# Two attention layers on one core: the value products of two score blocks in one bank, the output projections one a step, and the transposes of one residual block a step sooner

## The chip, the cores and the metric
One core of a Trainium2 chip runs the whole kernel. The metric is the device time in microseconds (us), from one launch; lower is better.

## The reference
The input x is 128 sequences of 128 tokens and 256 features, float32, with one 128x128 integer adjacency matrix for each sequence. Two layers follow each other:

```python
# layer 0: pre-norm transformer block, 8 heads of 32
nx = ln(x) * g1 + b1
scores = q @ k.T / sqrt(32) + where(adj > 0, 0.1 * adj * adj, -inf)
x1 = x + softmax(scores) @ v @ wo + bo
x2 = x1 + gelu(ln(x1) @ w1 + b1) @ w2 + b2          # 256 -> 1024 -> 256
# layer 1: graph attention, post-norm
scores = q @ k.T / sqrt(32), -inf where adj == 0
out = ln(x2 + softmax(scores) @ v @ Wo + bo) * gamma + beta
```

## The kernel before, in words
The 128 sequences go in 32 groups of 4 (GB). A software pipeline of 34 turns works on three groups at a time: stage A (attention of layer 0) on group i, stage M (the MLP of layer 0) on group i-1, stage C (layer 1) on group i-2. Turns 2 to 30 are one hardware loop of 29 turns; turns 0, 1, 31, 32 and 33 are written out, with some stages missing. `make_shapes` (L160) builds the turns and `Shape` (L73) the order of the work within one.

A turn has eight steps. Each step takes one score block (one sequence): steps 0 to 3 those of stage C (C0 to C3), steps 4 to 7 those of stage A (A0 to A3). What belongs to a score block is spread over several steps, on five engines:

- Scores: TensorE multiplies queries by keys in 32-row tiles (`make_scores` L1200, products at L1217). VectorE adds the mask and takes the negative maximum (L864), ScalarE exponentiates (L651), VectorE inverts the sums (`invert` L869) and GpSimd multiplies by them (`make_probs` L580, products at L585), in two halves of four heads, called g0 and g1.
- T, one step later: TensorE transposes the probabilities (`turn` L1221), half g0 before and half g1 after the output projection; ScalarE copies g0 out (L683), VectorE g1 (L923). A transpose waits for the GpSimd product of its half.
- V, two steps later: the products with the values in 32-column tiles (L1249), 16 records a block. ScalarE makes the rounded part (`heads_high` L685) and VectorE the remainder (`heads_low` L925), each 256 columns wide.
- W, also two steps later: the output projection in three passes (L1258), then residual and layer norm statistics on VectorE (`add_residual`, `measure`) and the reciprocal root on GpSimd (`rstd_of` L552).
- One step after W of a block of C: normalise on VectorE (`apply_norm` L949), gamma and beta on GpSimd (`finish` L566, L572 and L574), then SP stores the block (`store` L471).

Each engine has its own instruction queue and runs it in the order written in `body`; semaphores join them. TensorE's order in a step is: scores, V, the ops of `early` and `mid`, T g0, W, T g1, the ops of `ahead` (transposes of a residual block, XT), the ops of `fill`. Those tables (L105 to L111) hold the large products: K and Q of A and V of A in steps 0 to 2, up projection and first half of the down projection in step 3, second half in step 4, K, Q and V of C in steps 5 to 7. XT N, the transposes of the next group's normalised input, stand in step 7.

GpSimd's order in a step is at L579 to L625. At step 0 it first waits until all blocks of C of the turn before are stored, adds the bias of C to half a group (L593), then makes the g1 product of step 7's block, then the second half of the bias, then the g0 product of step 0's block:

```python
if k == 0 and s.c:
    wait(pool, stored, t.group_c * GB * 16)
    ...add_bias("C", drained[bank], number, 0, 1)
if k in s.open:
    make_probs(k - 1, 1)
...
for r in s.late.get(k, []):
    finish(t, r)
...
if k == 7 and s.a:
    add_bias("A", res_a_loaded, (t.group_a + 1) * 16, 1, 1)
rstd_of(t, s.lag.get(k, []))
```

Results of TensorE go through four PSUM banks in turn (`Turn.bank`), whose numbering follows TensorE's order.

Of the kernel before, what the change touches and what calls it, by code (L numbers as in the profile page):

```python
# [54 lines left out]
LOW_STEPS = {0: {5: [3], 6: [4], 7: [5]}, 1: {4: [6], 5: [7]}}  # L55
# [4 lines left out]
def lags(steps, pending, drain):  # L60

    by_step = {}
    for r, k in enumerate(steps):
        by_step[k] = ([("V", r - 2), ("W", r - 2)] if r >= 2 or pending else []) + (
            [("T", r - 1)] if r >= 1 or pending else [])
    last = len(steps) - 1
    tail = [("V", last - 1), ("T", last), ("W", last - 1), ("V", last), ("W", last)] if drain else []
    return by_step, tail  # L70


class Shape:  # L73
# [3 lines left out]
    def __init__(self, it, stages, following, before, drain):  # L77
# [13 lines left out]
        self.late, waiting = {}, [-3] if pending else []  # L91
        for k in self.steps:
# [6 lines left out]
                     if ((k - 1 in self.units and k - 1 != self.behind) if k != self.steps[0] else pending)]  # L99
# [9 lines left out]
        fill = {0: [("K", "A", 1)], 1: [("Q", "A", 1)], 2: [("V", "A", 1)],  # L109
# [3 lines left out]
        self.early = {k: [early[k]] for k in present if k in early}  # L113
        self.mid = {k: mid[k] for k in present if k in mid}
        self.fill = {k: fill[k] for k in present if k in fill}
        if before is None:

            self.early.update({5: [("XT", "N")], 6: [("K", "N", 1)], 7: [("Q", "N", 1)]})
            self.fill[1].append(("BIAS", 1))
            self.fill.update({5: [("K", "N", 0)], 6: [("Q", "N", 0)]})  # L120
            self.fill[7] = [("BIAS", 7)]
            self.tail = self.tail[:1] + [("BIAS", 2)] + self.tail[1:-1] + [
                ("V", "N", 0), self.tail[-1], ("V", "N", 1), ("BIAS", 3)]
# [14 lines left out]
        assert not self.looped or len(self.use) % BANKS == 0  # L138

# [30 lines left out]
class Turn:  # L170
# [28 lines left out]
    def normed_room(self, what):  # L199

        return (self.it + (what in "MN")) % 2
# [22 lines left out]
def build(nc, T, out):  # L224
    ctx = ExitStack()
    with ctx:
# [26 lines left out]
        probs_t = sb("probs_t", [P, H, P])  # L253
        heads_t = sb("heads_t", [P, 2, KC, P], F32R)
        piece_rooms = [sb(f"piece_room{i}", [P, 2, TOK]) for i in range(4)]
        scaled_rooms = [sb(f"scaled_room{i}", [P, 2, TOK]) for i in range(2)]
# [75 lines left out]
        scaled = [as_piece(scaled_rooms[n % 2][:, :, :]) for n in range(8)]  # L332
# [80 lines left out]
        def turned_rows(g):  # L413

            return probs_t[:, HC * g:HC * (g + 1)].rearrange("p (a h) n -> p a (h n)", a=2)
# [5 lines left out]
        def made(t, kind, what, i):  # L421
# [4 lines left out]
            return t.bank((kind, what, i), earlier=(what == "C"))  # L426
# [11 lines left out]
        def _(sp):  # L438
# [36 lines left out]
            def body(t):  # L475
# [26 lines left out]
                if s.c:  # L502
                    store(t, 0)
                    store(t, 1)
# [3 lines left out]
                if s.c:  # L508
                    store(t, 2)
# [11 lines left out]
        def _(pool):  # L521
# [11 lines left out]
            def scale_later(n):  # L533

                pool.wait_ge(piece_loaded[n], 16 * len(pieces[n][0]))
                if n in scaled_later:
                    pool.wait_ge(piece_done, EARLY_PIECES)
                    scale_part(nc.gpsimd, n).then_inc(later_scaled, 1)
# [37 lines left out]
            def body(t):  # L576
                s = t.s
                setup_over(pool, t)
                for k in range(STEPS):  # L579
# [16 lines left out]
                    for n in steps_of(LOW_STEPS, t).get(k, []):  # L596
# [18 lines left out]
                    rstd_of(t, s.lag.get(k, []))  # L615
                    if k == 3 and s.following and s.before is not None:
# [13 lines left out]
        def _(act):  # L630
# [49 lines left out]
            def turned(t, r):  # L680
                u, _, _ = t.unit(r)
                act.wait_ge(probs_turned, u * KC + 1)
                nc.scalar.activation(turned_rows(0), turned_columns(0), ACT.Copy).then_inc(turned_out0, 1)  # L683

            def heads_high(t, r):  # L685
                bank, number = t.bank(("O", r))
                act.wait_ge(filled[bank], number)
                nc.scalar.activation(heads_t[:, HI].rearrange("p c n -> p (c n)"), p_bank[bank][:, 0:KC * P],  # L688
                                     ACT.Copy).then_inc(high_made, 1)

            def body(t):
                s = t.s
                setup_over(act, t)
                for k in range(STEPS):
# [15 lines left out]
                    for _, r in only("T", lag):  # L710
                        turned(t, r)
                    if k in s.units and k != s.behind and not long:
                        exps(t, k, 1)
                    for op in s.ahead.get(k, []):
# [599 lines left out]
```

## Time and profile before

| what | value |
|---|---|
| time, median of 3 runs | 2192.55 us (2192.16 to 2194.01) |
| the profiled execution's own time | 2193.79 us |
| its span, first to last instruction | 2191.2 us |
| mean granted TensorE clock | 0.991 of full speed |
| TensorE busy | 2148.5 us, 98% |
| VectorE / ScalarE / GpSimd busy | 82% / 77% / 53% |
| one turn of the loop, from scores to scores | 66.12 us (1012.84 to 1078.96) |

The page gives busy time by engine and the costliest groups of instructions. Times in a timeline count from the span's start. In it a row is a run of equal instructions: start, time from the first start to the last end, engine, line, what is written and read, how many, and in brackets the idle time before it. TensorE's matmuls overlap, so the distance from one row's start to the next row's start is what a block of them costs, not its own duration.

### The profile page before, as it was taken

How to read it: one execution, taken by the hardware profiler on the slowest of the kernel's cores; microseconds unless marked ns; L12 is line 12 of the kernel's file. 1: busy time of each engine (PE TensorE's matmuls, PEld its weight loads, DVE VectorE, ACT ScalarE, POOL GpSimd, SP SyncE). 2: the span in 40 equal slices, each digit the busy share in tenths (PEclk: the TensorE clock that was granted, in tenths of full speed). 3: DMA queues.
4: the chain of work that ended last, by engine and by line, in shares of the span. 5: the costliest groups of instructions: out<-in, count | busy, mean ns of one | idle time of the engine just before them, and what ended most of it. 6: DMA issues, size and time to landing. Idle time of an engine off the chain costs nothing.

```text
span 2191.2 us, 58906 instructions
## 1 busy us (share of the span) xinstructions
PE 2148.5 (98%) x20300; PEld 1858.1 (85%) x20300; DVE 1798.5 (82%) x8414; ACT 1682.8 (77%) x5646; POOL 1153.9 (53%) x1266
## 2 busy tenths in 40 slices
PE   8899999999999999999999999999999999999986
PEld 6788888888888888888888888888888888888875
DVE  6588888888888888888888888888888888888774
ACT  5578777778877778877787877787877787877773
POOL 4345655455555455555455555455554456554454
PEclk9899999999999999999999999999999999999998
DMA  4010111001110101111101110101110101110000
GB/s 128 25 34 30 40 33 36 27 28 38 38 35 30 33 26 39 33 40 31 30 28 40 33 40 26 34 28 40 33 40 25 35 28 40 33 40 23 26 16 18
DMA packets 94308, 75.74 MB, mean 35 GB/s; under 512 B 8128, under 2 KB 93760, under 8 KB 94016
## 3 DMA queue, kind: packets, MB, share of 16 engines
q1 hardware_dynamic: 94016, 71.99, 10.9%
q8 instruction: 166, 2.72, 0.5%
q14 instruction: 126, 1.03, 0.2%
HBM read 55.20 MB, written 16.78 MB: 33 GB/s over the span
## 4 chain that ended last, share of the span: by engine, by line
PE 95%; issue 2%; DVE 1%; ACT 1%; POOL 0%; DMA 0%; SPq 0%; POOLq 0%; DVEq 0%
PE p_bank L1133 66%; PE p_heads L1230 10%; PE p_heads L1217 8%; PE p_bank L1249 7%; PE p_bank L1152 4%; ACT scores L651 1%; DVE normed L886 0%; DVE probs_t L923 0%; PE p_bank L1062 0%; DMA scores<-in_L_gnn_wk 0%; PE p_bank L1088 0%; POOL res_a L563 0%; SPq L442 0%; ACT normed L662 0%; ACT heads_t L688 0%
## 5 line engine op out<-in xcount | busy, mean ns | idle before, releaser
L651 ACT ACTIVATE scores<-scores,negmax 128x128 f32<-128x128 f32 x2048 | 793.7, 392 | 18.3 <-DVE negmax L864 18.0
L585 POOL TENSOR_TENSOR scores<-scores,inverse 128x512 f32<-128x512 f32 x512 | 541.2, 1062 | 329.9 <-DVE inverse L875 329.9
L651 ACT ACTIVATION_READ_ACCUMULATOR scores<-scores,negmax 128x1 f32 x2048 | 391.9, 191 | 0.0
L1133 PEld LDWEIGHTS p_bank<-w_down,hidden 128*128 128x128 f32 x3072 | 374.8, 190 | 8.6 <-issue 5.9
L1133 PE MATMUL p_bank<-w_down,hidden 128*128 128x256 f32 x3072 | 381.9, 284 | 0.0
L1133 PE MATMUL p_bank<-normed,w_up 128*128 128x512 f32 x1536 | 369.9, 397 | 2.2 <-DVE normed L886 2.2
L1133 PEld LDWEIGHTS p_bank<-normed,w_up 128*128 128x128 f32 x1536 | 284.9, 189 | 67.5 <-issue 8.6
L1230 PE MATMUL p_heads<-ident,scores 128*128 128x128 f32 x2048 | 312.7, 276 | 6.9 <-DVE negmax L864 3.5
L864 DVE CUSTOM_DVE_ANT_0 scores<-p_heads,adj_a 128x128 f32<-128x128 f32 x1024 | 235.2, 286 | 45.2 <-issue 45.2
L674 ACT ACTIVATE p_bank<-p_bank,ready_cols 128x512 f32<-128x512 f32 x256 | 169.5, 662 | 132.2 <-PE p_bank L1133 126.5
L1230 PEld LDWEIGHTS p_heads<-ident,scores 128*128 128x128 f32 x2048 | 241.5, 141 | 32.9 <-DVE negmax L864 10.5
L864 DVE CUSTOM_DVE_ANT_0 scores<-p_heads,adj_c 128x128 f32<-128x128 f32 x1024 | 233.2, 286 | 36.1 <-issue 36.1
L1133 PE MATMUL p_bank<-w_o,heads_t 128*128 128x256 f32 x1536 | 246.5, 296 | 1.9 <-DVE heads_t L929 1.9
L910 DVE TENSOR_TENSOR hidden<-p_bank,hidden 128x512 fp32r<-128x512 f32 x256 | 177.1, 692 | 63.0 <-ACT hidden L678 57.1
L688 ACT ACTIVATE heads_t<-p_bank 128x256 fp32r<-128x256 f32 x256 | 98.3, 384 | 166.7 <-PE p_bank L1249 166.7
L683 ACT ACTIVATE probs_t<-p_heads 128x512 f32<-128x512 f32 x256 | 149.9, 585 | 89.3 <-PE p_heads L1230 89.3
L530 POOL TENSOR_TENSOR rstd_A<-spread_A,half 128x4 f32<-128x4 f32 x32 | 32.5, 1017 | 352.2 <-DVE spread_A L765 352.2
L1133 PE MATMUL p_bank<-normed,w_k 128*128 128x512 f32 x768 | 211.4, 412 | 5.1 <-DVE normed L886 3.9
L1133 PE MATMUL p_bank<-normed,w_q 128*128 128x512 f32 x768 | 210.5, 410 | 0.0
L1133 PE MATMUL p_bank<-w_v,normed 128*128 128x256 f32 x1536 | 209.8, 287 | 0.0
L1133 PEld LDWEIGHTS p_bank<-w_o,heads_t 128*128 128x128 f32 x1536 | 199.7, 191 | 3.0 <-DVE heads_t L929 2.8
L1133 PEld LDWEIGHTS p_bank<-w_v,normed 128*128 128x128 f32 x1536 | 186.7, 189 | 12.6 <-issue 12.5
(117 smaller groups left out, 3698.1 us busy)
## 6 DMA issues: line engine op xcount, KB each, us to landing
res_a<-in_x SPq DMA_DIRECT2D x32, 512.0 KB, 3.8
out<-res_c SPq DMA_DIRECT2D x128, 128.0 KB, 1.7
x_in<-in_x SPq DMA_DIRECT2D x31, 512.0 KB, 3.8
adj_a<-in_adj SPq DMA_DIRECT2D x32, 256.0 KB, 2.9
adj_c<-in_adj SPq DMA_DIRECT2D x32, 256.0 KB, 2.8
piece_room<-in_L_gnn_w SPq DMA_DIRECT2D x2, 512.0 KB, 7.5
x_two<-in_x SPq DMA_DIRECT2D x1, 512.0 KB, 5.4
res_c<-in_L_gnn_w SPq DMA_DIRECT2D x1, 512.0 KB, 6.3
```

The lines of the kernel that those rows point to most:

```text
L585: nc.gpsimd.tensor_tensor(rows_g, rows_g, inverse[:, step % 2, heads].unsqueeze(2).broadcast_to([P, HC, P]), ALU.mult).then_inc(probs_made, 1)
L651: last = nc.scalar.activation(scores[:, k % 2, h], scores[:, k % 2, h], ACT.Exp, scale=-1.0, bias=negmax[:, k % 2, h:h + 1], accum_out=tot ...
L674: nc.scalar.activation(src[:, :], src[:, :], ACT.Gelu, bias=ready_cols[:, 8 + j:9 + j]).then_inc(gelu_made, 1)
L683: nc.scalar.activation(turned_rows(0), turned_columns(0), ACT.Copy).then_inc(turned_out0, 1)
L688: nc.scalar.activation(heads_t[:, HI].rearrange("p c n -> p (c n)"), p_bank[bank][:, 0:KC * P], ACT.Copy).then_inc(high_made, 1)
L864: nc.vector.tensor_tensor_reduce(out=scores[:, k % 2, slot], in0=score_columns(c, j), in1=adj[stage][:, b, :], scale=1.0, scalar=LARGEST, ...
L910: nc.vector.tensor_tensor(hidden[:, j, LO, :], src[:, :], hidden[:, j, HI, :].bitcast(F32), ALU.subtract).then_inc(drained[bank], 1)
L1133: last = nc.tensor.matmul(dst, stationary(i), moving(j), start=(n == 0), stop=(n == total_n - 1))
L1152: last = nc.tensor.transpose(dst[:, b * P:(b + 1) * P], src[:, b, c * P:(c + 1) * P], ident[:, :])
L1217: last = nc.tensor.matmul(score_columns(c, j), queries[room(t, stage)][rows_j, c, tokens], keys[room(t, stage)][rows_j, c, tokens], start= ...
L1230: last = nc.tensor.transpose(turned_columns(g)[:, n // 2, (n % 2) * P:(n % 2 + 1) * P], scores[:, par, HC * g + n, :], ident[:, :])
L1249: last = nc.tensor.matmul(dst[HD * j:HD * (j + 1), c * P:(c + 1) * P], values[room(t, stage)][:, b, h * HD:(h + 1) * HD], probs_t[:, slot_ ...
```

## The change
The value products of two blocks are made one after the other in the steps 1, 3, 5 and 7 into one bank, 512 columns wide, and rounded and subtracted at that width; `probs_t` and `heads_t` become double. W is done for the blocks of `W` in the table:

| step | before: V, W | after: V | after: W |
|---|---|---|---|
| 0 | A2 | none | A1 |
| 1 | A3 | A2, A3 | A2, A3 |
| 2 | C0 | none | none |
| 3 | C1 | C0, C1 | C0 |
| 4 | C2 | none | C1 |
| 5 | C3 | C2, C3 | C2 |
| 6 | A0 | none | C3 |
| 7 | A1 | A0, A1 | A0 |

(The A blocks of steps 0 and 1 are those of the turn before.) `finish` and the norm of a block of C move with its W: C3's from step 6 to step 7. XT N moves from step 7 to step 6, both halves of V of A stand in `early` of step 2, ScalarE evacuates XT before the second half of its exponentials, and SP stores block 1 behind the load of `res_a`. At the ends: V of C for the last group moves from turn 32 into the first step of turn 33; in turn 0 V of A moves behind the first scores; in turn 1 GpSimd scales and splits the last two weight pieces in steps 2 and 3 instead of 4 and 5; the drained tails are reordered. GpSimd's order in a loop turn is otherwise the same.

```diff
+    by_step = {k: [] for k in steps}
     for r, k in enumerate(steps):
-        by_step[k] = ([("V", r - 2), ("W", r - 2)] if r >= 2 or pending else []) + (
-            [("T", r - 1)] if r >= 1 or pending else [])
+        by_step[k] += [("T", r - 1)] if r >= 1 or pending else []
+        by_step[k] += [("W", -3)] if r == 0 and pending else []
+        if r % 2 and (r >= 3 or pending):
+            by_step[k] += [("V", (r - 3, r - 2)), ("W", r - 3)]
+            if r == 1:
+                by_step[k] += [("W", r - 2)]
+            elif r < len(steps) - 1:
+                by_step[steps[r + 1]] += [("W", r - 2)]
-    tail = [("V", last - 1), ("T", last), ("W", last - 1), ("V", last), ("W", last)] if drain else []
+    tail = [("W", last - 2), ("V", (last - 1,)), ("T", last), ("W", last - 1), ("V", (last,)), ("W", last)] if drain else []
...
-                      7: [("XT", "N")] * (a and following and before is not None)}
-        early = {1: ("Q", "A", 0), 2: ("V", "A", 0), 4: ("DOWN", 1), 6: ("Q", "C", 0), 7: ("V", "C", 0)}
+                      6: [("XT", "N")] * (a and following and before is not None)}
+        early = {1: [("Q", "A", 0)], 2: [("V", "A", 0), ("V", "A", 1)], 4: [("DOWN", 1)], 6: [("Q", "C", 0)],
+                 7: [("V", "C", 0)]}
...
+        if it == NG:
+            del self.early[7], self.fill[7]
+        if it == NG + 1:
+            self.early[0], self.fill[0] = [("V", "C", 0)], [("V", "C", 1)]
         if before is None:
+            del self.early[2]
+            self.fill[4] = [("V", "A", 0), ("V", "A", 1)]
...
-            def heads_high(t, r):
-                bank, number = t.bank(("O", r))
+            def heads_high(t, units):
+                bank, number = t.bank(("O", units))
                 act.wait_ge(filled[bank], number)
-                nc.scalar.activation(heads_t[:, HI].rearrange("p c n -> p (c n)"), p_bank[bank][:, 0:KC * P],
+                nc.scalar.activation(heads_part(HI, units), p_bank[bank][:, 0:len(units) * KC * P],
                                      ACT.Copy).then_inc(high_made, 1)
...
+                    if k == 2 and second_turn(t):
+                        scale_later(6)
...
+                    if k == 3 and second_turn(t):
+                        low_later(6)
+                        scale_later(7)
+                        low_later(7)
```

## Rows read from the trace of the kernel before
**Rows 1.** Windows: one turn; busy us of each engine, granted clock, DMA share, GB/s.
```profile
1012.84:1078.96 66.12, 66.08 (x633) 57.38 (x633) 55.91 (x263) 52.25 (x178) 35.50 (x39) 1.00 0.11 33
```
**Rows 2.** Timeline, TensorE: from step 6 to step 0 of the next turn.
```profile
1032.37 0.60 PE L1230 MATMUL p_heads<-ident,scores 128*128 128x128 f32 x4
...
1034.29 0.73 PE L1217 MATMUL p_heads<-keys_a,queries_a 32*128 32x128 f32 x16
...
1038.59 1.04 PE L1152 MATMUL p_bank<-ident,x_in 128*128 128x128 f32 x8
1039.38 1.62 PE L1133 MATMUL p_bank<-w_v,normed 128*128 128x256 f32 x12
1040.94 0.73 PE L1217 MATMUL p_heads<-keys_c,queries_c 32*128 32x128 f32 x16
1041.60 0.64 PE L1249 MATMUL p_bank<-probs_t,values_a 128*32 128x128 f32 x16
1042.17 1.65 PE L1133 MATMUL p_bank<-normed,w_k 128*128 128x512 f32 x6
...
1044.81 0.60 PE L1230 MATMUL p_heads<-ident,scores 128*128 128x128 f32 x4
```
**Rows 3.** Timeline, TensorE, turn 1: step 4, and a wait after it.
```profile
83.53 0.73 PE L1217 MATMUL p_heads<-keys_a,queries_a 32*128 32x128 f32 x16
84.19 6.02 PE L1133 MATMUL p_bank<-w_down,hidden 128*128 128x256 f32 x48
...
94.16 0.66 PE L1152 MATMUL p_bank<-ident,x_two 128*128 128x128 f32 x4 [3.52 <-DVE x_two L917]
```
**Rows 4.** Timeline, ScalarE: step 7 of the same turn.
```profile
1035.66 0.38 ACT L688 ACTIVATE heads_t<-p_bank 128x256 fp32r<-128x256 f32 x1 [0.57 <-PE p_bank L1249]
...
1037.96 0.58 ACT L683 ACTIVATE probs_t<-p_heads 128x512 f32<-128x512 f32 x1
```
**Rows 5.** The page, part 5: VectorE subtractions, 512 and 256 wide; busy us, mean ns.
```profile
L910 DVE TENSOR_TENSOR hidden<-p_bank,hidden 128x512 fp32r<-128x512 f32 x256 | 177.1, 692 | 63.0 <-ACT hidden L678 57.1
...
L929 DVE TENSOR_TENSOR heads_t<-p_bank,heads_t 128x256 fp32r<-128x256 f32 x256 | 107.2, 419 | 24.3 <-ACT heads_t L688 24.2
```
**Rows 6.** Timeline, GpSimd: steps 5 to 0 of the same turns.
```profile
1026.75 1.12 POOL L585 TENSOR_TENSOR scores<-scores,inverse 128x512 f32<-128x512 f32 x1 [0.34 <-DVE inverse L875]
1027.83 0.73 POOL L572 TENSOR_TENSOR res_c<-res_c,gamma 128x256 f32<-128x256 f32 x1
...
1029.32 1.28 POOL L563 TENSOR_TENSOR res_a<-res_a,row_bias 128x512 f32<-128x512 f32 x1
...
1031.08 2.10 POOL L585 TENSOR_TENSOR scores<-scores,inverse 128x512 f32<-128x512 f32 x2
...
1037.87 1.04 POOL L585 TENSOR_TENSOR scores<-scores,inverse 128x512 f32<-128x512 f32 x1 [0.64 <-DVE inverse L875]
1038.87 1.29 POOL L563 TENSOR_TENSOR res_a<-res_a,row_bias 128x512 f32<-128x512 f32 x1
1040.31 0.55 POOL L530 TENSOR_TENSOR rstd_M<-spread_M,half 128x1 f32<-128x1 f32 x1
1040.82 1.27 POOL L563 TENSOR_TENSOR res_c<-x_two,row_bias 128x512 f32<-128x512 f32 x1
...
1042.91 1.04 POOL L585 TENSOR_TENSOR scores<-scores,inverse 128x512 f32<-128x512 f32 x1 [0.81 <-DVE inverse L875]
```
**Rows 7.** Timeline, GpSimd: beta of a block, then a bias that waits for its store.
```profile
2145.26 0.72 POOL L574 TENSOR_TENSOR res_c<-res_c,beta 128x256 f32<-128x256 f32 x1
2147.77 2.54 POOL L563 TENSOR_TENSOR res_c<-x_two,row_bias 128x512 f32<-128x512 f32 x2 [1.78 <-DMA out<-res_c]
```
**Rows 8.** Timeline, TensorE: rows after waits, in turns 0, 32 and 33.
```profile
52.21 1.08 PE L1230 MATMUL p_heads<-ident,scores 128*128 128x128 f32 x4 [1.40 <-issue]
...
2103.40 0.73 PE L1217 MATMUL p_heads<-keys_c,queries_c 32*128 32x128 f32 x16 [1.72 <-DVE probs_t L923]
...
2158.73 0.73 PE L1217 MATMUL p_heads<-keys_c,queries_c 32*128 32x128 f32 x16 [1.91 <-DVE negmax L864]
```

More of the change, by code:

```diff
@@ L88, in __init__ @@
         self.lag, self.tail = lags(self.steps, pending, drain)
-        self.late, waiting = {}, [-3] if pending else []
+        self.pending = pending
+        self.late, waiting = {}, []
         for k in self.steps:
@@ L138, in __init__, with use_units @@
         assert not self.looped or len(self.use) % BANKS == 0
+    def use_units(self, r):
+        return [use[1] for use in self.use if use[0] == "O" and use[1][0] == r]
     def number(self, ops):
@@ L199, in normed_room @@
     def normed_room(self, what):
-        return (self.it + (what in "MN")) % 2
+        return (self.it + (what in "MN" or not self.s.m and self.s.c)) % 2
     def high(self, key):
@@ L331, in build @@
                                         piece_rooms[3][:, :, :])]
-        scaled = [as_piece(scaled_rooms[n % 2][:, :, :]) for n in range(8)]
+        scaled = [as_piece(scaled_room[:, :, :]) for n in range(8)]
         w1, w2 = w_view(L0 + "w1"), w_view(L0 + "w2")
@@ L425, in made, with second_turn @@
                 return t.bank((kind, "N", i), earlier=True)
-            return t.bank((kind, what, i), earlier=(what == "C"))
+            return t.bank((kind, what, i), earlier=(what == "C" and not (kind == "V" and t.it == NG + 1)))
+        def second_turn(t):
+            return t.s.before is not None and t.s.before.before is None
         def steps_of(table, t):
@@ L508, in body @@
                 if s.c:
+                    store(t, 1)
                     store(t, 2)
@@ L595, in body @@
                         make_probs(k - 1, 1)
-                    for n in steps_of(LOW_STEPS, t).get(k, []):
+                    for n in LOW_STEPS.get(k, []) if s.before is None else []:
                         if n > 3:
@@ L711, in body @@
                         turned(t, r)
+                    for op in s.ahead.get(k, []) if not long else []:
+                        evacuate(t, op)
                     if k in s.units and k != s.behind and not long:
                         exps(t, k, 1)
-                    for op in s.ahead.get(k, []):
+                    for op in s.ahead.get(k, []) if long else []:
                         evacuate(t, op)
@@ new lines, in project @@
+            def project(t, r):
+                for units in t.s.use_units(r):
+                    bank, number = t.bank(("O", units))
+                    pe.wait_ge(drained[bank], number)
+                bank, dst = take(t, ("W", r))
+                w = weight[weights_of[t.unit(r)[1]][3]]
+                three_passes(dst[:, 0:D], [(lambda i, c=c: heads_t[:, i, parity(r), c, :], lambda j, c=c: w[:, j, c, :])
+                                           for c in range(KC)]).then_inc(filled[bank], 1)
@@ L1236, in lagging @@
+            def lagging(t, op, which):
                 if op == "T":
                     for g in range(2):
-                        turn(t, r, g)
+                        turn(t, which, g)
                 if op == "V":
-                    bank, dst = take(t, ("O", r))
-                    pe.wait_ge(turned_out0, u + 1)
-                    pe.wait_ge(turned_out1, u + 1)
-                    if b == 0:
-                        for i in range(2):
-                            pe.wait_ge(*drained_bank(*made(t, "V", stage, i)))
@@ L1246, in lagging @@
[L1246 to L1260 removed]
+                    value_products(t, which)
```

93 lines of the change are left out of this document (48 added, 45 removed).

## The prediction
> **What bounds the kernel now.** I read the windows first, one turn of the loop: TensorE is busy 66.08 of 66.12 us, at granted clock 1.00, which is the upper of its two levels, 2.4 GHz; VectorE, ScalarE and GpSimd are busy 55.91, 52.25 and 35.50 us [rows 1]. So in the 29 loop turns nothing but TensorE's own queue sets the time, and every microsecond that this queue waits is paid in full. Then I read TensorE's timeline row by row for what a block of each kind costs (start to next start), and at last the timelines of GpSimd and ScalarE for how long before its use each result is ready. The reader should look in the last for slack: a product of the probabilities that ends shortly before the transpose that needs it.
>
> **What TensorE saves.** A block of value products costs 0.57 us (1041.60 to 1042.17) [rows 2]. Eight 128-column transposes take 1.04 us in their row and four take 0.60, so one more costs 0.11; a block is four rounds of four tiles side by side, 0.44 us if they ran at that pitch. The missing 0.13 is the change of tile shape and is paid once a block. A pair then costs 0.57 + 0.44 = 1.01 us and not 1.14. Where V goes from a step altogether, the scores are followed by the next full-size product after 0.66 us (83.53 to 84.19) [rows 3], the same 0.66 as from scores to V (1040.94 to 1041.60) [rows 2], so V is taken out whole. Four pairs a turn: 4 x 0.13 = 0.54 us with the unrounded starts. Bounds: nothing, if each block keeps its own 0.13; 4 x 0.2 = 0.8, if the pair also hides some of what surrounds it. I take 0.54, since the rows give it directly. W, T and XT keep their number and widths; joining or parting them shifts less than 0.1 us a turn either way, which I set to nothing. Over 31 turns that have pairs: -17 us.
>
> **What the other engines save.** ScalarE and VectorE do four wide roundings for eight narrow ones. On ScalarE a 256-wide copy takes 0.38 and a 512-wide one 0.58 [rows 4]; on VectorE 0.42 and 0.69 [rows 5]. All of it lies beside TensorE, so it buys nothing; but each wide one is longer, and what is queued behind it comes later.
>
> **What becomes late: T g1 in step 0.** Let zero be the start of the scores of step 7 (1034.29). Before, T g1 of step 0 starts at 10.52 (1044.81) [rows 2]. The product of GpSimd that it needs (g1 of step 7's block) starts at 8.62 (1042.91) and ends at 9.66 [rows 6]: slack 0.86. After the change TensorE comes sooner: XT N has left step 7 (-0.79, 1038.59 to 1039.38 [rows 2]), the pair is +0.44, V has left step 0 (-0.57): it wants T g1 at 10.52 - 0.92 = 9.60.
> GpSimd comes later, step by step [rows 6, 4]:
> the g0 product of step 7 starts at 3.58 (1037.87); it waits for the inverse of sums whose exponentials stand behind `heads_high` on ScalarE. The pair ends 0.44 later and its copy is 0.20 longer (0.58 for 0.38): 4.22.
> It occupies 1.00 (1037.87 to 1038.87): 5.22.
> `finish` of C3 is new here, since C3's W moved from step 5 to step 6: gamma and beta occupy 1.49 (1027.83 to 1029.32): 6.71.
> The bias of A, 1.29: 8.00. The reciprocal root, 0.51 (1040.31 to 1040.82): 8.51. Before there was 0.15 of idle time ahead of it, now none.
> In step 0 GpSimd waits until C3 is stored. From the end of beta (2145.98) to the bias that its store releases (2147.77) it is 1.79 us [rows 7]: 6.71 + 1.79 = 8.50, by chance the same moment.
> The bias of C, 1.27, stands ahead of the product: 9.78. The product, 1.04: 10.82, plus some 0.03 for the semaphore.
> T g1 waits 10.85 - 9.60 = 1.25 us. The 0.82 us that GpSimd had waited for the inverse before its product [rows 6] are used up in this count. Behind T g1 on TensorE stand K of A, the scores of step 1 and everything else, with no other work to fill the gap. Bounds: 0.6 if GpSimd's small instructions and the store are quicker than in these rows; 2.0 if ScalarE, which now evacuates XT N before the second half of its exponentials, gets late too. The store's size is the least certain term.
> The Trainium skill, "DMA: Bandwidth & Descriptors", in "Anatomy of one DMA — SWDGE (gpsimd) path", gives a fixed cost of about 2.0 us a DMA, most of it the wait for the write to be confirmed; the trace has 1.79 us with beta's hand-over in it [rows 7], for a DMA issued by SP. With 2.0 the wait would be an estimated 1.5 us and the sum 6 us more; the measured one is used.
>
> **What becomes late: T g1 in step 6.** GpSimd's queue from the g0 product of step 5 (1026.75) to the g1 product at 1031.08 has no gap: product, `finish`, bias of A, root, product. That first product waits for an inverse behind the masks and `heads_low`, now 0.69 - 0.42 = 0.27 longer [rows 5], so the g1 product ends at 1032.12 + 0.27 = 1032.39. T g1 stood at 1032.37 [rows 2], with 0.25 of slack, and moves by +0.44 - 0.57 to 1032.24. That is 0.15 of wait, and up to 0.4 where K of C in step 5 no longer waits for its transposes. I take 0.3. Both waits come in 30 turns: the first at the starts of turns 3 to 32, the second in turns 2 to 31. Together 30 x 1.55 = +46 us.
>
> **The edits of W, XT M and V of A** are covered: W of a pair's first block stands 1.9 us behind the pair (a K, Q or V product and T g0), against 1.3 us for the two wide roundings; XT M reaches the up projection behind scores and a pair, 1.7 us, for the roundings of two banks.
>
> **The ends.** In turn 1 TensorE waits 3.52 us for the down projection's sum [rows 3], because ScalarE's exponentials stand behind weight pieces that GpSimd scales in step 4; scaled two steps sooner they don't: -3.5, and an estimated -1.5 for the products behind it, which after such gaps at the ends can run at the lower clock (T in 1.08 for 0.60 at 52.21 [rows 8]). V of C placed behind the first scores of turn 33 covers the 1.91 us wait [rows 8]: -1.9; V of A likewise in turn 0, where I take a little less: -1.5. The drained tail now has W of one more block, so after the last root GpSimd finishes four blocks and not three: +1.5 (1.49 as above). Sum -7, between -14 and +2.
>
> **Sum.** Against the profiled execution's own time, 2193.8 (its span is 2191.2): 2193.8 - 17 + 46 - 7 = 2216. The median of the runs shown is 1.2 us lower, so 2215 us.
>
> **Rivals.**
> A, faster: GpSimd is ready in time. The time is 2192.6 - 17 - 7 = 2168 us. For it: GpSimd is idle for 30 of 66 us of a turn [rows 1]. Against: that idle time lies in steps 3 and 4; between step 7's g0 product and step 0's g1 product it has 0.97 us of it (0.15 and 0.82), while 1.49 of `finish` and 0.64 of delay are added. It decides if that product ends 9.6 us after the scores of step 7.
> B, in between: the two waits add up to 0.4 to 1.0 us a turn; the change breaks even at 24 / 30 = 0.8. 2180 to 2199, middle 2190.
> C, much slower: the new gap lowers TensorE's clock in each turn. After 1.40 us of waiting four transposes took 1.08 us in place of 0.60 (52.21) [rows 8]: if some 2.5 us a turn are lost so, 2215 + 75 = 2290. Against: after waits of 1.72 and 1.91 us the scores ran in 0.73 us, as at full clock (2103.40, 2158.73) [rows 8], and here 9 us of dense products stand ahead of the gap.
> [...]
> D, the pair doesn't save: each block keeps its 0.13. Then 2215 + 17 = 2232.
>
> **Chances.** Forecast 0.66, A 0.15, B 0.10, C 0.05, D 0.04. The measurement tells no change from a change within 0.2%, 4.4 us: 2188 to 2197. Faster: A and a third of B, 0.18. Same: half of B, 0.05. Slower: the rest, 0.77. The forecast's own range is 2199 to 2234. To leave out no more than A and C the range starts in B, at 2180, and ends at 2236, with D in it.
>
> **What would show it.** In TensorE's timeline: rows of 32 value products costing 1.01 us, and steps 0, 2, 4 and 6 without any (D: 1.14). Rows of transposes in step 0 with about 1.25 us of idle time, in step 6 with 0.3; in the waits, GpSimd's probabilities as a releaser that isn't there now. A turn of 67.1 us, not 66.12 (A: 65.6). On GpSimd gamma and beta between step 7's product and the bias of A, and the bias of C of step 0 at 8.5 us after the scores of step 7. Granted clock 1.00 over a turn; below 0.97 would be C. The first 100 us some 6 us shorter. I would be wrong if GpSimd's bias of C started before 7.2 us, or if another engine waited instead.

## The result, and the profile after

| | before | after |
|---|---|---|
| time, median | 2193.39 us (2192.16 to 2194.01) | 2254.04 us, 5 runs (2248.59 to 2258.19) |
| ratio, 95% interval | | 1.0268 (1.0252 to 1.0284) |
| span of the profiled execution | 2191.2 us | 2255.7 us (its own time 2258.2) |
| mean granted TensorE clock | 0.991 | 0.985 |
| a turn | 66.11 to 66.16 us, the last of them 65.24 | 67.57 us in 19 of 30, 66.30 in one, 68.3 to 70.4 in ten |

The change makes the kernel 61 us slower. The forecast said slower by 22, and its range (2180 to 2236) doesn't hold the result. The profiled execution of the kernel after was the slowest of its five, so the spans differ by 64.5 us and the medians by 60.7.

One thing has to be put right first. The text ahead of the prediction says that turns 2 to 30 are one hardware loop. They are not: `make_shapes` (L160) writes all 34 turns out one after the other. That matters below: the profile shows 165 fetches of instructions, 16 KB each, spread over the whole span (queue q8).

The windows of the kernel after, in the columns of [rows 1]: a common turn, a long one, and eight microseconds of the long one.

```profile
998.24:1065.81 67.57, 66.03 (x633) 57.64 (x633) 55.78 (x258) 51.74 (x173) 35.42 (x40) 1.00 0.11 33
314.07:383.93 69.86, 67.55 (x634) 58.67 (x633) 55.78 (x258) 51.74 (x173) 35.44 (x40) 0.98 0.10 32
318.00:326.00 8.00, 6.29 (x63) 4.78 (x64) 4.19 (x18) 3.35 (x14) 5.35 (x6) 0.79 0.16 55
```

TensorE was busy all of the turn before (66.08 of 66.12); now 1.54 us of the common turn are idle. Its timeline, from step 6 to step 0 of the next turn, answers to [rows 2]:

```profile
1056.78 0.63 PE L1267 MATMUL p_heads<-ident,scores 128*128 128x128 f32 x4
...
1059.60 0.73 PE L1255 MATMUL p_heads<-keys_a,queries_a 32*128 32x128 f32 x16
1060.26 1.08 PE L1285 MATMUL p_bank<-probs_t,values_a 128*32 128x128 f32 x32
1061.27 1.65 PE L1171 MATMUL p_bank<-w_v,normed 128*128 128x256 f32 x12
...
1063.11 0.96 PE L1171 MATMUL p_bank<-w_o,heads_t 128*128 128x256 f32 x6
1063.90 0.60 PE L1267 MATMUL p_heads<-ident,scores 128*128 128x128 f32 x4
...
1065.81 0.73 PE L1255 MATMUL p_heads<-keys_c,queries_c 32*128 32x128 f32 x16
...
1068.32 0.95 PE L1171 MATMUL p_bank<-w_o,heads_t 128*128 128x256 f32 x6
1070.68 0.63 PE L1267 MATMUL p_heads<-ident,scores 128*128 128x128 f32 x4 [1.41 <-issue]
1071.07 1.64 PE L1171 MATMUL p_bank<-normed,w_k 128*128 128x512 f32 x6
```

The pair costs 1.01 us (1060.26 to 1061.27). W costs 0.79 (1063.11 to 1063.90), so TensorE wanted T g1 of step 0 at 1069.11, 9.51 after step 7's scores; it starts at 11.08, 1.57 late. GpSimd's timeline of the same stretch answers to [rows 6]:

```profile
1063.83 1.12 POOL L617 TENSOR_TENSOR scores<-scores,inverse 128x512 f32<-128x512 f32 x1 [1.29 <-DVE inverse L916]
1064.92 0.74 POOL L604 TENSOR_TENSOR res_c<-res_c,gamma 128x256 f32<-128x256 f32 x1
1065.73 0.73 POOL L606 TENSOR_TENSOR res_c<-res_c,beta 128x256 f32<-128x256 f32 x1
1066.42 1.29 POOL L595 TENSOR_TENSOR res_a<-res_a,row_bias 128x512 f32<-128x512 f32 x1
1067.67 0.55 POOL L561 TENSOR_TENSOR rstd_M<-spread_M,half 128x1 f32<-128x1 f32 x1
1068.31 1.28 POOL L595 TENSOR_TENSOR res_c<-x_two,row_bias 128x512 f32<-128x512 f32 x1
1069.55 1.04 POOL L617 TENSOR_TENSOR scores<-scores,inverse 128x512 f32<-128x512 f32 x1
```

Seven operations in a row with no gap over 0.1 us, and T g1 waits for the last. In a long turn the same two places (GpSimd, then TensorE) read:

```profile
317.35 1.26 POOL L595 TENSOR_TENSOR res_c<-x_two,row_bias 128x512 f32<-128x512 f32 x1 [0.87 <-DMA out<-res_c]
```
```profile
319.71 0.66 PE L1267 MATMUL p_heads<-ident,scores 128*128 128x128 f32 x4 [2.18 <-issue]
320.10 2.83 PE L1171 MATMUL p_bank<-normed,w_k 128*128 128x512 f32 x6
```

Here GpSimd waits 0.87 us for the store of the fourth block of C, TensorE waits 2.18, and then the six products of K take 2.83 us in place of 1.64 and the scores of step 1 behind them 1.05 in place of 0.73: the granted clock over 318 to 326 us is 0.79, so part of that stretch ran at the lower level of 1.2 GHz.

**Where the 64.5 us of span went**, from the starts of the scores: before turn 2, -2.6 (115.27 to 112.66); turns 2 to 31, +58.7, which is +42.3 for turns longer by 1.45 and +16.4 more in ten of them; turn 32 between its scores 0 and 3, +8.2 (15.03 to 23.23); the rest +0.2.

The ten long turns are just those whose store lands late. The fourth block's store is issued 0.68 us after the scores of step 0 every time. In turns 3 to 31 it lands 1.75 us later in 19 and takes 2.47 to 3.22 in ten; in turn 32 it is late too (2.85). In six of the ten the turn is longer by exactly what the store is late, within 0.02 (landed 3.22, so 1.47 late: turn 69.04, 1.47 longer). In the other four it is 1.5 longer still (landed 2.54, 0.79 late: turn 69.85, 2.28 longer), which is K and the products behind it at the lower clock.

### The profile page after: what moved, and what is told of

Its sections match the earlier page's. It is cut to its first block, busy times and chain, and to the rows that moved or that the text cites. A ratio compares the mean times of both kernels' runs of the same rounds, so it can differ in the third digit from the quotient of the medians.

```text
span 2255.7 us, 58407 instructions
## 1 busy us (share of the span) xinstructions
PE 2157.7 (96%) x20300; PEld 1873.5 (83%) x20300; DVE 1798.8 (80%) x8289; ACT 1666.3 (74%) x5521; POOL 1153.1 (51%) x1266
## 3 DMA queue, kind: packets, MB, share of 16 engines
q14 instruction: 124, 1.02, 0.2%
## 4 chain that ended last, share of the span: by engine, by line
PE 92%; issue 4%; DVE 1%; ACT 1%; POOL 0%; POOLq 0%; DVEq 0%; ACTq 0%
PE p_bank L1171 64%; PE p_heads L1267 10%; PE p_heads L1255 7%; PE p_bank L1285 6%; PE p_bank L1190 4%; ACT scores L689 0%; DVE probs_t L964 0%; DVE scores L905 0%; POOL res_c L604 0%; DVE normed L927 0%; DVE heads_t L969 0%; POOL res_c L606 0%; ACT normed L700 0%; DVE res_c L979 0%; DVE stats_C L797 0%
## 5 line engine op out<-in xcount | busy, mean ns | idle before, releaser
L1171 PE MATMUL p_bank<-w_o,heads_t 128*128 128x256 f32 x1536 | 239.0, 295 | 3.5 <-DVE heads_t L969 3.5
L964 DVE COPY probs_t<-p_heads 128x512 f32<-128x512 f32 x256 | 176.7, 690 | 60.3 <-PE p_heads L1267 58.7
L1171 PE MATMUL p_bank<-normed,w_k 128*128 128x512 f32 x768 | 217.0, 420 | 3.4 <-DVE normed L927 3.4
L1171 PE MATMUL p_bank<-w_v,normed 128*128 128x256 f32 x1536 | 203.5, 285 | 0.0
```

The lines of the kernel that those rows point to most:

```text
L964: nc.vector.tensor_copy(turned_rows(r, 1), turned_columns(1)).then_inc(turned_out1, 1)
L1171: last = nc.tensor.matmul(dst, stationary(i), moving(j), start=(n == 0), stop=(n == total_n - 1))
```

## The experiments

"The turn" is the common turn in the middle of the kernel. All runs are compared with the kernel before on their own chip.

**e1: the product ahead of the bias.** GpSimd makes the g1 product of step 7's block before it waits for the store.

```diff
+                    if k in s.open:
+                        make_probs(k - 1, 1)
                     if k == 0 and s.c:

                         wait(pool, stored, t.group_c * GB * 16)
                         bank, number = t.bank(("DOWN", 1), earlier=True)
                         add_bias("C", drained[bank], number, 0, 1)
-                    if k in s.open:
-                        make_probs(k - 1, 1)
```

> The changed kernel, with one edit: in step 0 GpSimd makes the g1 product of step 7's block before it waits for the stores and adds the bias of C. Theory Q (GpSimd's queue): the product starts when the root ends, 8.6 us after the scores of step 7, and T g1 waits 0.2 in place of 1.56 us; but the bias of C now ends 1.0 us later, VectorE's normalisation of block A0 waits for it with the copy of T g1 behind it, and the scores of step 1 wait for that copy: 0.8 to 1.2 us come back there. A turn of 67.1 to 67.4 us (67.57 now); the turns with a late store lose most of their excess, since the bias has 0.9 us to spare. Time 2230 to 2240 us. Rival (TensorE is held by the product alone): a turn of 66.2 us, time 2205 us.

Measured: 2252.07 us, ratio 1.0263 (1.0248 to 1.0278), turn 67.85. A miss: T g1 is only 0.2 late, but the scores of step 1 now wait 1.58, more than the 0.8 to 1.2 expected. From the waits of this run (who waited for whom; total us, times, longest):

```profile
PE p_heads L1255 <- DVE probs_t L964: 54.3, 34, 3.0
...
DVE x_two L811 <- POOL res_c L595: 46.9, 31, 2.0
```

VectorE's norm of a residual block overwrites `x_two`, which the bias of C must have read; behind the norm on VectorE stands the copy of T g1's bank, and the next scores need that bank. So two chains hang on the same late moment of GpSimd, 31 times each; mending one of them gives nothing that these runs can tell (2 us, with ranges that overlap).

**e2: no wait for the store.** The sum of C goes to a weight room that is free by then, so GpSimd no longer waits for the store, and VectorE's move of the first block of C, in a later step, waits for it instead.

```diff
-                x, src = (res_c, x_two) if stage == "C" else (res_a, res_a)
+                x, src = (sum_c, x_two) if stage == "C" else (res_a, res_a)
...
-                        wait(pool, stored, t.group_c * GB * 16)
...
+                if stage == "C" and b == 0:
+                    wait(dve, stored, t.group(r) * GB * 16)
```

> The changed kernel, with the sum of x2 and the bias of C written to a free weight room and not over the block being stored, so that GpSimd waits for no store in step 0 (VectorE waits for it in step 3, long after). Order of the queues as in the changed kernel. Theory Q: the common turn stays at 67.5 us, since the root ends only 0.1 us before the store lands; what goes is the excess of the turns with a late store (15.5 us in all in the profiled run) and about 2 us of the wait in turn 32: time 2233 to 2240 us. Rival S (the store is what TensorE waits for): the whole 1.56 us a turn goes, 66.0 us a turn, time 2190 us.

Measured: 2230.46 us, ratio 1.0165 (1.0150 to 1.0181). Turns 3 to 30 are all 67.42 or 67.43; no long one is left.

```profile
982.90:1050.33 67.43, 66.02 (x634) 57.65 (x634) 55.77 (x258) 51.70 (x173) 35.36 (x40) 1.00 0.11 33
```

23.6 us of the 61 hang on the store and only 0.14 us of each common turn: with a store of 1.75 GpSimd is released at about the moment at which it comes free anyway.

**e3: loads behind the store.** SP waits for the store before it issues the loads of `adj_a` and `x_in`, which otherwise follow it within 1.4 us.

```diff
                 if s.c:
                     store(t, 3)
+                    sp.wait_ge(stored, (t.group_c + 1) * GB * 16)
```

> The changed kernel, with one edit: SP waits until C3 is stored before it issues the loads of adj_a and x_in, which now are issued 0.4 and 0.9 us behind that store. Theory V (a store's landing time varies by itself: in the trace of the kernel before 30 of 128 stores took over 2.0 us from issue, most with no load behind them): nothing changes, about a third of the turns keep their excess, time 2248 to 2258 us. Rival L (the loads delay the store): no late store in step 7, no turn over 67.6 us but for turn 32, time 2236 to 2240 us.

Measured: 2254.01 us, ratio 1.0270 (1.0252 to 1.0287), the same long turns at the same places. The loads don't make the late stores. They cost every store a little: without them behind it the punctual one takes 1.69 us, not 1.75, and the common turn is 67.51.

**e4: the late finish in the kernel before.** Gamma and beta of the fourth block of C in step 7 instead of step 6, nothing else.

```diff
                     for r in s.late.get(k, []):
-                        finish(t, r)
+                        if not (k == 6 and s.a and s.c):
+                            finish(t, r)
+                    if k == 7 and s.a and s.c:
+                        finish(t, 3)
```

> The kernel before, with one edit: gamma and beta of C3 in step 7 and not in step 6 (what the change does to GpSimd, without what it does to TensorE, ScalarE and VectorE). Theory Q: the bias of C starts 7.9 us after the scores of step 7, the g1 product ends at 10.2, T g1 stands at 10.5: the common turn keeps its 66.1 us. Theory V adds: a store that lands over 0.3 us late is now paid for, 9 to 15 us in all, time 2201 to 2208 us. Rival (the work put into step 7 is paid by itself): 1.2 us a turn, 2230 us. Rival L: 2193 us, since here the x load comes 4 us after that store.

Measured: 2197.82 us, ratio 1.0024 (1.0014 to 1.0034). That is less than the 2201 to 2208 expected. The common turn stays 66.12; five turns are 0.2 to 0.8 longer, and turn 32 between its scores 0 and 3 takes 19.25 for 15.03. The later finish alone is nearly free, because in the kernel before TensorE wants T g1 0.92 us later.

**e5: e2, and the finish deferred.** GpSimd's gamma and beta of the fourth block go behind all its work of step 0 of the next turn.

```diff
                     for r in s.late.get(k, []):
-                        finish(t, r)
+                        if not (k == 7 and r == 3 and not s.drain):
+                            finish(t, r)
...
                     rstd_of(t, s.lag.get(k, []))
+                    if k == 0 and s.before is not None and s.before.c and not s.before.drain:
+                        finish(t, 3, t.group_c - 1)
```

> The changed kernel with GpSimd's bias of C in a room of its own (as in e2), and the finish of the fourth block of C (the product with g1 is unchanged; its scale, gamma, beta and the store behind them) taken out of step 7's list on GpSimd and put behind all that GpSimd does in step 0 of the next turn. What is computed is the same. Theory Q (the cost of the turn is TensorE's wait for T g1's source in step 0, and that is late only because GpSimd's gamma and beta of the fourth block stand ahead of it): with some 1.9 us of work taken from ahead of it the bias of C starts early enough, the wait of 1.3 to 1.5 in step 0 is gone, and the turn falls from 67.43 to 66.0 (the wait of 0.3 in step 6 stays); 2230.5 less 31 times 1.4 gives 2187 (2184 to 2191). Rival R (another wait stands right behind, as in e1: VectorE's norm or the copies of the probabilities): the turn stays above 67.0 and the time at 2215 or more. The difference of the two is what one projection a step with pairs of value products costs beyond GpSimd's order.

Measured: 2198.70 us, ratio 1.0018 (1.0007 to 1.0028), turn 66.38. T g1 of step 0 is on time, but only 1.05 of the 1.4 us came back: the scores of step 1 now wait 0.33 for VectorE's copy.

**e6: e5, and the bias of A a step later.**

```diff
-                    if k == 5 and s.a:
+                    if k == (5 if s.before is None else 6) and s.a:
                         add_bias("A", res_a_loaded, (t.group_a + 1) * 16, 0, 1)
```

> e5, and in the full turns the bias of A's first half is done by GpSimd in step 6 and not in step 5. The change brought a wait of 0.3 for T g1 in step 6 as well, which I put to GpSimd's queue of step 5. Theory Q: it goes, the turn falls from 66.0 to 65.7, below the 66.12 of the kernel before by what the pairs save (4 times 0.13), and the time to 2178 (2174 to 2182). Rival R: the bias of A is wanted by the norm in step 6 itself, a wait of the same length takes its place, and the time stays at e5's within 3 us.

Measured: 2187.58 us, ratio 0.9971 (0.9961 to 0.9981), turn 66.03. The edit gives 0.35 a turn, the wait of step 6, as expected; the level is 0.35 too high, as in e5.

**e7: e6, and the last turn reordered.** GpSimd's part of it; on VectorE the norms stand ahead of the moves of the third and the fourth block.

```diff
-                        rstd_of(t, s.tail)
-                        for r in s.last:
-                            finish(t, r)
+                            rstd_of(t, tail_w[:1])
+                            finish(t, s.last[0])
+                            finish(t, s.last[1])
+                            rstd_of(t, tail_w[1:2])
+                            finish(t, s.last[2])
+                            rstd_of(t, tail_w[2:])
+                            finish(t, s.last[3])
```

> e6, and in the last turn VectorE's norms and GpSimd's finishes of the four blocks are taken in the order in which their projections end, in place of all roots first and all finishes behind. Theory: at the end of the changed kernel four finishes stand in a row behind the last projection (from last W to end 11.2 us), of which two can be done while TensorE still works: 3 to 4 us less than e6, 2172 to 2176, and faster than the kernel before by 0.8 to 1 per cent. Rival: the last finish waits for its own root and norm and not for the finishes ahead of it; then it is e6's time within 1 us.

Measured: 2187.14 us, ratio 0.9970 (0.9959 to 0.9981): a miss, no difference from e6 that these runs can tell. The 0.35 that e5 and e6 lack is found in this trace. VectorE, then GpSimd, then TensorE, in step 0:

```profile
1037.93 1.43 DVE L824 TENSOR_SCALAR x_two<-res_a,moments_M,rstd_M 128x256 f32<-128x256 f32 x1
1039.29 0.41 DVE L994 TENSOR_TENSOR res_a<-p_bank,res_a 128x256 f32<-128x256 f32 x1
1039.62 0.68 DVE L977 COPY probs_t<-p_heads 128x512 f32<-128x512 f32 x1
```
```profile
1037.93 1.29 POOL L596 TENSOR_TENSOR piece_room<-x_two,row_bias 128x512 f32<-128x512 f32 x1
```
```profile
1040.45 0.73 PE L1273 MATMUL p_heads<-keys_c,queries_c 32*128 32x128 f32 x16 [0.34 <-DVE probs_t L977]
```

The norm takes 1.43 us where its like takes 0.40, and it ends 0.14 after GpSimd's bias, which started with it. The copy comes late by that, and the scores wait 0.34.

**e8: the second bias behind the product.** e7, and on GpSimd:

```diff
-                    if k == 0 and s.c:
-                        add_bias("C", drained[bank], number, 1, 1)
                     if k in s.units and k != s.behind:
                         make_probs(k, 0)
+                    if k == 0 and s.c:
+                        add_bias("C", drained[bank], number, 1, 1)
```

> e7, and in step 0 GpSimd's second bias of C (1.29 us) stands behind its product with g0 (1.04) instead of ahead of it. In e7's turn one wait of TensorE is left: 0.34 before the scores of step 1, for VectorE's copy of the probabilities of T g1, which stands behind a norm that took 1.43 (starting with GpSimd's second bias, at 1037.93, and ending 0.14 behind it) where the same norm elsewhere takes 0.40. Theory N (such a norm, with its source and its target in SBUF, can't run beside a GpSimd instruction and ends when that ends): now the product is beside it, 0.25 shorter, the norm takes about 1.18, the wait falls from 0.34 to 0.1 and the turn from 66.07 to 65.82; time 2187 less 8 = 2179 (2176 to 2183). Rival W (the norm is long for a reason of its own, such as the blocks it writes): the norm stays 1.43, the turn 66.07, the time 2187.

Measured: 2173.54 us, ratio 0.9900 (0.9880 to 0.9919), turn 65.66. VectorE and GpSimd:

```profile
1030.65 0.40 DVE L824 TENSOR_SCALAR x_two<-res_a,moments_M,rstd_M 128x256 f32<-128x256 f32 x1
```
```profile
1029.65 2.30 POOL L618 TENSOR_TENSOR scores<-scores,inverse 128x512 f32<-128x512 f32 x2
```

Better than expected: the norm begins in the moment between two GpSimd operations, takes 0.40, and now GpSimd pays: its two products take 2.30 us, where two in a row take 2.10 in [rows 6]. The rival (long by itself) falls: the same norm is short in all turns here but one, where it takes 1.02 and the turn 65.97. In the profiles of the two kernels and the twelve variants, every one of the 384 norms into `x_two` that took over 0.6 us ended 0.15 to 0.16 us after a GpSimd operation.

**e9: the norm behind the copy.** e7, with VectorE's norm of step 0 behind its move of W and its copy of T g1.

```diff
-                    if k < 2 and s.m and s.pending:
+                    if k == 1 and s.m and s.pending:
                         apply_norm(t, -1, k)
...
                     for _, r in only("T", lag):
                         turned(t, r)
+                    if k == 0 and s.m and s.pending:
+                        apply_norm(t, -1, k)
```

> e7, and in step 0 VectorE's norm of the pending block (1.43 beside GpSimd's bias) stands behind its move of W and its copy of T g1's bank, in place of ahead of them. GpSimd is as in e7. Theory: nothing of step 0 waits for the norm, the wait of 0.34 is gone whole, the turn is 65.73, and 31 turns give 2187 less 10.5 = 2176.5 (2174 to 2180). Rival: the norm now stands ahead of step 1's masks beside GpSimd's product, comes late there, and the turn stays within 0.1 of 66.07.

Measured: 2171.93 us (2169.07 to 2173.40), before 2197.59 on this chip, ratio **0.9886 (0.9868 to 0.9903)**: the fastest of all, 1.1% under the kernel before and below the 2174 to 2180 expected. TensorE waits nowhere in the turn:

```profile
1028.33:1093.97 65.64, 65.64 (x634) 57.61 (x633) 55.56 (x258) 51.61 (x173) 35.45 (x40) 1.00 0.11 34
```

**e10: e9 without e7's edit of the last turn.**

> e9 without e7's edit of the last turn, so that the two kernels differ in the last turn alone (e6 and e7, which do too, came out at 2187.58 and 2187.14, with profiled starts that differ by 2.8 us the other way). Theory (the tail is 2.5 to 3 us shorter, as the two profiles show from the last turn on, and the starts differ by chance from one execution to the next): 2.5 to 3 us above e9, 2179 to 2182. Rival (the tail's gain is no gain in most executions): within 1 us of e9.

Measured: 2174.41 us (2173.85 to 2175.67), 2.5 above e9, the difference that was expected (the time itself is below the 2179 to 2182 said); the ranges don't overlap. The two profiled starts of turn 2 lie 1.6 us apart (107.65 and 109.24), and between e6 and e7 2.8 (107.14 and 109.94), e7's the later. So the start varies by some microseconds between executions and can hide a gain of this size in one profile. The traces show two parts of it: the first K of turn 0 begins between 13.9 and 16.8 us, and K behind a wait in turn 1 takes 2.90 us in some executions and 1.62 in others, at the two levels of the clock. What decides either was not settled, nor why e7 and e6 came out alike.

**e11 and e12: where the instructions are fetched.** The changed kernel with 128 and with 256 more TensorE instructions ahead of its first turn. What led to them is the view of the DMA queues, here of the kernel after around two stores. First one that lands in time (247.1 to 249.9 us):

```profile
q1 hardware_dynamic: 647, 0.39, 49.1%
...
out<-res_c SPq DMA_DIRECT2D x1, 128.0 KB, 1.7
```

and one that doesn't (384.5 to 387.3 us):

```profile
q1 hardware_dynamic: 144, 0.13, 14.7%
q8 instruction: 1, 0.02, 2.5%
...
out<-res_c SPq DMA_DIRECT2D x1, 128.0 KB, 2.9
```

Columns: queue and kind: packets, MB, share of the time of 16 engines; in the last row the store, KB, us from issue to landing. A single packet of 16 KB, an instruction fetch, is in flight beside the late store; 2.5% of 16 engines for 2.8 us is 1.1 us of one engine.

```diff
             pe.wait_ge(setup_vector, 1)
+            ones = spread_bv.rearrange("p a n -> p (a n)")
+            for _ in range(32):                      # 64 in e12
+                nc.tensor.matmul(p_bank[BANKS - 1][:, 0:32], ident[:, :], ones[:, 0:32], start=True, stop=True)
             keep_busy(4)
```

> The changed kernel with 128 more TensorE instructions ahead of its first turn (64 pairs of weight load and matmul with 32 columns, results unused, while the first loads are under way). The turns are untouched. In the trace of the changed kernel the fourth block's store lands 1.75 us after its issue in 20 of the 30 turns that follow one, and 2.47 to 3.22 in 10 (groups 2, 3, 4, 9, 10, 15, 16, 18, 22, 28); these 10 are just the 10 long turns. In 8 of them a packet of 16 KB of the instruction queue q8 starts 0.3 to 1.1 us after the issue, and in groups 2 and 18 one of 8 KB of q14 is in flight; no store without such a packet is over 2.0. 166 packets of 16 KB are 42,500 instructions of 64 bytes, as many as TensorE's matmuls and weight loads, so a fetch comes every 256 of them; the pattern comes back every 6 turns. Theory F (a store is late when it meets a fetch of instructions): 128 instructions are half a fetch, so the fetches move by half their distance, which is 3 turns of the pattern, and the late stores by 16 KB become groups 0 or 1, 6, 7, 12, 13, 18 or 19, 25 and 26, while 3, 4, 9, 10, 15, 16, 22 and 28 land in 1.75; the number stays 8 to 12 and the time 2254 to 2262 with the added work. Rival T (the late stores hang on the loads, the addresses or the group): the groups stay 3, 4, 9, 10, 15, 16, 22, 28.

> The same with 256 instructions more ahead of the first turn (128 pairs), a whole fetch. Theory F: the fetches fall where they fell before, one number later, and the late groups are again 3, 4, 9, 10, 15, 16, 22, 28 (and 29 behind the last full turn), as in the changed kernel and unlike the run with 128. Rival S (any added work at the start shifts the set in some way, by time and not by the count of instructions): the set differs from the changed kernel's. Time 2256 to 2268 with the added work at the start.

Measured, the groups whose fourth store took over 2.0 us, the last full turn's included:

| kernel | beside a fetch of 16 KB | beside one of 8 KB |
|---|---|---|
| after | 3 4 9 10 15 16 22 28 29 | 2 18 |
| e11, +128 | 0 1 6 7 12 13 18 19 25 | 2 15 |
| e12, +256 | 3 4 9 10 15 16 22 28 29 | 2 18 |

Half a fetch moves the set by three turns (26, also expected, lands in time), a whole fetch brings it back. The text expected for e11 says 20 of 30 punctual in the kernel after; with group 29 it is 19 of 30. The queue rows of e11 around the stores of group 0 and of group 3, which have changed places with those of the kernel after:

```profile
q1 hardware_dynamic: 672, 0.40, 46.4%
q8 instruction: 1, 0.02, 2.4%
...
out<-res_c SPq DMA_DIRECT2D x1, 128.0 KB, 2.9
```
```profile
q1 hardware_dynamic: 731, 0.46, 60.0%
...
out<-res_c SPq DMA_DIRECT2D x1, 128.0 KB, 1.7
```

The times, 2266.28 and 2282.56 us (two runs each), are above what was expected: the added work costs more at the start than I allowed (turn 2 starts at 121.53 and 134.78, not 112.66), and in e12 seven long turns have products at the lower clock, not four. Over the profiled executions of the two kernels and the twelve variants, 1226 stores had no instruction packet beside them (in flight 0.3 to 1.75 us behind the issue), and none of them took over 2.0 us; of 460 beside a 16 KB packet 316 did, and of 106 beside one of 8 KB alone 32. So a fetch is needed for a late store, but doesn't always make one.

## Why the prediction was wrong, step by step

- **What bounds the kernel; the pair.** Right. The pair is 1.01 us; a turn without waits is 65.64 (e9), 0.48 under 66.12, where 0.54 was said.
- **T g1 in step 0, mechanism.** Right, and in the order told: the g0 product at 4.23 (said 4.22), gamma, beta, bias of A and root in a row, the bias of C at 8.71 (8.50), T g1 at 11.08 (10.85). The wait is 1.57 for 1.25: a g0 product of 1.09 for 1.00, a TensorE that comes 0.09 sooner, and 0.14 by the store (e2).
- **T g1 in step 6.** Right: 0.35 for 0.3 (e5 against e6). Both waits together: 1.93 a turn for 1.55, 11 us over 29 turns.
- **The failed step is the price of the store**: "From the end of beta (2145.98) to the bias that its store releases (2147.77) it is 1.79 us". That is one row for 30 stores, and with it the store ended at 8.50, just when GpSimd came free anyway, so the sum paid nothing for it. It is right for 19 of them and 0.7 to 1.5 short for the other 11, of which nine meet a fetch of 16 KB in q8, TensorE's by e11 and e12, and two one of 8 KB in q14, whose engine no run shows. The text called this "the least certain term" and yet let it only be quicker. By e2, taking the store out of GpSimd's way is worth 23.6 us: 16.4 in the ten long turns (about 10 by lateness, 6 by the clock), 0.14 in each of the others, and some 3 of the 8 us of turn 32. With the store out of the way the time, 2230.46, lies inside the range that was stated. The information was there: in the trace of the kernel before, 30 of its 128 stores take over 2.0 us, up to 3.7, harmless where they stood.
- **The ends**, the second step that failed: said -7, between -14 and +2; measured +5.8. The start gave 2.6 of 6.5 by these two profiles, but they are a poor pair: turn 2 begins at 115.27 and 112.30 in the two profiles with the old start (before, e4) and at 105.94 to 112.66 in the ten with the new one (after, e1 to e3, e5 to e10), the kernel after being the latest of the ten and their median 108.05. So the start gave 4 to 7, about what was said, and it is turn 32 that failed. In the profile after, turn 1's wait fell only to 1.44 (it was 3.52, [rows 3]), and turn 0 has a new one of 3.21, both for VectorE; TensorE's timeline after:

```profile
31.19 1.97 PE L1190 MATMUL p_bank<-ident,x_two 128*128 128x128 f32 x8 [3.21 <-DVE x_two L811]
...
93.48 0.66 PE L1190 MATMUL p_bank<-ident,x_two 128*128 128x128 f32 x4 [1.44 <-DVE x_two L958]
```

Turn 32 went the wrong way by 8.2, which I had not priced: its store is late too, and what follows the wait is at the lower clock. The store is the smaller part: without a wait for it (e2) the stretch takes 19.95 us of the 23.23, and the kernel before with the late finish alone (e4) takes 19.25, both with rows at the lower clock. How the other 4.9 divide was not tested.

```profile
2159.95 1.07 PE L1267 MATMUL p_heads<-ident,scores 128*128 128x128 f32 x4 [2.80 <-issue]
2161.89 1.24 PE L1255 MATMUL p_heads<-keys_c,queries_c 32*128 32x128 f32 x16 [0.87 <-DVE probs_t L964]
2163.06 1.94 PE L1285 MATMUL p_bank<-probs_t,values_a 128*32 128x128 f32 x32
```

- **The rivals.** A and B fell with the common turn, D with the pair. C (the clock falls in each turn) fell in that form: after the wait of 1.41 us K takes 1.64 and the turn's granted clock is 1.00. In 4 of the 10 longer waits of the full turns it came true, 1.5 us each, and in turn 32.
- **Sum**, by the two profiles: 22 said; +11 for the waits a little longer, +16 for the long turns, +2 for the pairs, +13 for the ends (8 of it turn 32) make 64.

**Can the change pay?** Yes, with the queues of GpSimd and VectorE mended: e9 keeps its pairs and its single projections and is 1.1% under the kernel before. Of its 25.7 us the reordered last turn gives 2.5 (e10), which is no part of the change; the turn gives 0.48 each time (66.12 to 65.64). The same edits in the kernel before were not run; its TensorE had 0.04 us of idle time a turn to win by them. The change as made was a good order for TensorE joined to a GpSimd queue that had no room for it.

## What to carry to other kernels

Before moving work of the bounding engine, count each helper's queue up to the moment of use, and look for a second chain on the same late moment: e1 mended one of two and gained nothing that its runs can tell. A wait for a DMA is priced with the spread of its landing times over the whole trace, not by one row. And an edit that makes a kernel slower may be half of one that makes it faster; the trace tells which queue has to give.

## What the runs showed of the hardware

- **An instruction fetch delays a store.** 128 KB stores with no instruction packet beside them take 1.69 to 1.94 us (1226 stores, median 1.72); of 460 beside a 16 KB packet 316 take 2.0 to 3.7. In this kernel, written out, there is such a packet every 13.7 us (165 in 2255.7). The set of late stores follows the count of TensorE's instructions (e11, e12). The Trainium skill, "Runtime: NRT & Kernel Launch", section "Instruction fetch mechanics", says that code comes in blocks of 256 instructions through a DMA queue of the sequencer's own; the trace agrees (q8, 165 packets, 2.70 MB) and adds that other transfers pay for it. That the store's share on one of the 16 DMA engines queues behind the packet is my reading and was not shown by itself.
- **A VectorE norm from SBUF to SBUF and a GpSimd operation exclude each other**: 1.43 (e7) and 0.99 us (e9) in place of 0.40, ending 0.15 after GpSimd's in all 384 long ones; begun first, it holds up GpSimd (e8: two products in 2.30 us for 2.10). VectorE's operations that read PSUM beside GpSimd kept their times (0.42 and 0.69 in e8), and so did its statistics, which read SBUF (0.42). The Trainium skill, "Trainium Architecture — The Big Picture", section "What this means for kernel authors", calls the port pair that the two share an exclusive lock; by that rule this is what one should see, and the trace agrees.
- **The clock** fell to its lower level in 4 of the 10 turns with longer waits (2.18 us, with K at 2.83 behind it), in none of the 19 with 1.41, and not in the one with the longest wait, 2.87. What decides among the ten stays open.
